# A two-layer graph network on one core: first loads issued within the preceding stage, last node tiles finished on VectorE, padding tile left out, loops written out

## What is computed

```
# layer 0: graph convolution with self loops
deg  = segment_sum(w, dst) + 1 ;  dis = rsqrt(deg)
agg  = segment_sum(x[src] * dis[src] * w, dst)      # sum0, one row per node
out0 = relu(dis * ((agg + dis * x) @ W0) + b0)
x1   = layernorm(x + out0)
# layer 1: continuous-filter convolution on edges (i = src, j = dst)
filt = (softplus(f_ij @ Wf1 + bf1) - log 2) @ Wf2 + bf2
m    = products of (x1[j] @ Win), direction Y and filt, times edge weight
agg1 = segment_sum(m @ W1, i)                       # sum1
S, V = (softplus(agg1_scalar) - log 2) @ W2_s , agg1_vector
out  = layernorm(x1 + [S, V])
```

## Time and profile before

| | us |
|---|---|
| median of three runs | 1147.39 |
| the profiled execution | 1145.88 |
| its span in the trace | 1144.1 |

### The profile page before, as it was taken

One profiled execution on the slowest core, in us unless ns is written; L12 is line 12 of the kernel. 1 busy time (PEld: TensorE's weight loads), 2 busy tenths in 40 slices (PEclk: granted clock), 3 DMA queues, 4 the chain that ended last, 5 costly groups with the idle time before them and its releaser, 6 DMA issues.

```text
span 1144.1 us, 20007 instructions
## 1 busy us (share of the span) xinstructions
PE 963.5 (84%) x4768; PEld 744.5 (65%) x4768; DVE 812.6 (71%) x2537; ACT 651.0 (57%) x1472; POOL 602.4 (53%) x692
## 2 busy tenths in 40 slices
PE   7789989999838999999994599999999999544443
PEld 7667767767627888777773477777777777333332
DVE  8888868768607787878784366666666666268887
ACT  1268867877723555555555244444445444168887
POOL 3337788888743666666665455665665664300000
PEclk9989989889978999999997699999999999855555
DMA  9989999999977999999995789999999997599994
GB/s 353 419 270 247 246 238 248 232 230 235 236 161 222 315 310 310 309 308 314 310 311 210 225 173 205 196 198 205 195 200 205 195 202 156 70 359 362 362 359 167
DMA packets 153397, 287.95 MB, mean 252 GB/s; under 512 B 17850, under 2 KB 54366, under 8 KB 153342
## 3 DMA queue, kind: packets, MB, share of 16 engines
q1 hardware_dynamic: 104254, 192.95, 49.0%
q0 software_dynamic: 35840, 83.91, 38.7%
q10 hardware_dynamic: 13248, 10.49, 2.8%
HBM read 138.88 MB, written 148.41 MB: 251 GB/s over the span
## 4 chain that ended last, share of the span: by engine, by line
PE 37%; ACT 10%; issue 9%; DVE 7%; DMA 3%; ACTq 2%; POOL 1%; DVEq 1%; SPq 1%; POOLq 0%
PE bank L1133 6%; PE bank L1144 5%; PE bank L1102 4%; DVE node_mem L880 3%; PE bank L1142 3%; PE bank L1154 3%; PE bank L1156 3%; PE bank L1157 3%; PE bank L1126 2%; ACT G_hi L618 2%; PE bank L1106 2%; ACTq L619 2%; ACT node_mem L632 2%; PE bank L1134 2%; PE bank L1140 2%
## 5 line engine op out<-in xcount | busy, mean ns | idle before, releaser
L517 POOL DMA_INDIRECT sum<-R_mem,l_sidx x80 | 127.5, 1594 | 127.1 <-ACT R_mem L646 75.0
L462 POOL DMA_INDIRECT sum<-R_mem,sidx_all x80 | 130.9, 1636 | 71.4 <-DMA sum<-zeros 34.9
L493 POOL TENSOR_TENSOR node_mem<-node_mem,G_mem 128x512 f32<-128x512 f32 x80 | 103.2, 1290 | 91.7 <-ACT node_mem L626 91.7
L1102 PE MATMUL bank<-W0h,G_hi 128*128 128x512 f32 x320 | 134.2, 419 | 0.9 <-ACT G_hi L618 0.7
L1102 PE MATMUL bank<-W0l,G_hi 128*128 128x512 f32 x320 | 126.0, 394 | 0.0
L626 ACT ACTIVATE node_mem<-node_mem 128x512 f32<-128x512 f32 x80 | 50.7, 633 | 118.1 <-DVE node_mem L880 118.1
L925 DVE SCALAR_TENSOR_TENSOR edge_mem<-edge_mem,Y,bank 128x128 f32<-128x128 f32 x240 | 72.5, 388 | 57.3 <-ACT edge_mem L660 57.3
L660 ACT COPY edge_mem<-bank 128x256 f32<-128x256 f32 x80 | 29.8, 372 | 134.3 <-PE bank L1144 134.3
L1027 PE MATMUL bank<-G_hi,M_mem 128*128 128x512 f32 x200 | 89.0, 445 | 17.4 <-ACT R_mem L561 15.9
L509 POOL DMA_INDIRECT G_mem<-x_d,dst_i x80 | 79.4, 992 | 36.8 <-issue 23.2
L1170 PE MATMUL bank<-ident,node_mem 128*128 128x128 f32 x80 | 27.5, 447 | 82.9 <-DVE node_mem L953 82.9
(11 more groups left out here) (177 smaller groups left out, 2765.6 us busy)
## 6 DMA issues: line engine op xcount, KB each, us to landing
filt_d<-node_mem SPq DMA_DIRECT2D x40, 512.0 KB, 5.0
node_mem<-sum SPq DMA_DIRECT2D x80, 256.0 KB, 3.6
G_mem<-x SPq DMA_DIRECT2D x80, 256.0 KB, 3.6
x_d<-node_mem SPq DMA_DIRECT2D x80, 256.0 KB, 2.5
node_mem<-filt_d SPq DMA_DIRECT2D x80, 256.0 KB, 4.5
sum<-zeros SPq DMA_DIRECT2D x34, 512.0 KB
sum<-node_mem SPq DMA_DIRECT2D x80, 192.0 KB, 2.8
edge_mem<-sum SPq DMA_DIRECT2D x15, 512.0 KB, 5.6
```

The lines of the kernel that those rows point to most:

```text
L462: pool.indirect_dma_start(sum0, bass.IndirectOffsetOnAxis(ap=sidx[:, t:t + 1], axis=0), R[t % 8][:, :], None, compute_op=ALU.add).then_inc ...
L493: pool.tensor_tensor(res[a], res[a], xl[a], ALU.add).then_inc(n_sum, 1)
L517: pool.indirect_dma_start(sum1, bass.IndirectOffsetOnAxis(ap=l1_sidx[:, t:t + 1], axis=0), R3[t % 8][:, :], None, compute_op=ALU.add).then ...
L1102: pe.matmul(bank[4 + a][:, :], zT_hi[a][:, c * P:(c + 1) * P], w[:, c, :], start=(c == 0 and w is W0h), stop=False)
```

## The change

- `TR` = 79 tiles are gathered, scattered and run through `nodes0` and `edges1`. The first edge stage keeps its 20 groups: TensorE, ScalarE and VectorE still work on tile 79, GpSimd neither gathers nor scatters it. `sum0`, `sum1` and `x1_d` are 128 rows shorter, and the last of the 42 zero stores has half its size.
- The first eight loads of `x` for the node stage are issued by SyncE before it waits for the filter stores and the scatters; they wait for the last low part (`e_lo`), when the `G0` buffers are free.
- The first four `trow3` and `filt` loads of the second edge stage are issued within SyncE's node stage, at step TR + 4 = 83, ahead of the store of tile 71.
- The first eight `xs` loads of the last stage are issued when the last product of the second edge stage is made, before the wait for its scatters.
- Tiles 75 to 78 of the node stage: after L880 VectorE itself applies ReLU and adds `x` in one instruction; ScalarE's ReLU and GpSimd's add are left out for them, and their statistics are taken one step earlier.
- The four DMAs of L637 are issued at steps 7, 15, 23 and 31 of ScalarE's node stage.
- `nodes0` and `edges1` are straight-line code in all steps on all engines. `held` increments nothing where its value is a number, which it now always is.
- In `edges1` tile 78 has no partner: TensorE sums it alone and ScalarE copies it one step earlier.

```diff
+TR = (N + P - 1) // P
+TAIL = TR - 4
+NR = TR * P
...
-def live(s, lag, steps=T):
+def live(s, lag, steps=TR):
...
         def held(eng, s, value):
-            if not isinstance(value, int) or value > 0:
+            if isinstance(value, int):
+                wait(eng, s, value)
+            else:
...
-            for j in range(NZ, 42):
+            for j in range(NZ, 41):
                 sp_.dma_start(zero_rows(j), zeros[:, :]).then_inc(s_zero0, 16)
+            sp_.dma_start(sum0[41 * 256:, :], zeros[:, 0:D]).then_inc(s_zero0, 16)
...
-            sp_.wait_ge(e_scat, 16 * T)
+            sp_.wait_ge(e_lo, T)
+            for t in range(8):
+                sp_.dma_start(xl[t], rows(x, t)).then_inc(n_xl[t], 16)
             for k in range(4):
                 sp_.wait_ge(w_st[k], 16 * (T // 8))
+            sp_.wait_ge(e_scat, 16 * TR)
...
                     sp_.dma_start(sl[a], rows(sum0, s)).then_inc(n_sl[a], 16)
-                    held(sp_, n_sum, s - 7)
-                    sp_.dma_start(xl[u], rows(x, s)).then_inc(n_xl[u], 16)
+                    if s >= 8:
+                        sp_.wait_ge(n_sum, s - 7)
+                        sp_.dma_start(xl[u], rows(x, s)).then_inc(n_xl[u], 16)
+                if s == TR + 4:
+                    for g in range(4):
+                        trow_in(g)
+                    sp_.wait_ge(n_tr, TR)
+                    for t in range(4):
+                        filt_in(t)
...
-            skewed(sp_, nodes0, 12, 16, unroll=8)
...
+            for s in range(TR + 12):
+                nodes0(s, s % 8)
...
-            sp_.wait_ge(f_scat, 16 * T)
+            sp_.wait_ge(f_m, K_PROD * TR)
+            for s in range(8):
+                sp_.dma_start(xs[s], node_pair(x1_d, s, 0, C)).then_inc(g_xs[s], 16)
+            sp_.wait_ge(f_scat, 16 * TR)
...
                 for n, j in enumerate((3, 2, 1, 0)):
                     t = 4 * g + j
+                    if t >= TR:
+                        continue
...
-                if live(s, 4):
+                if live(s, 4, TAIL):
                     t, a = s - 4, (u - 4) % 8
                     pool.wait_ge(n_rel, t + 1)
                     pool.tensor_tensor(res[a], res[a], xl[a], ALU.add).then_inc(n_sum, 1)
...
                     act.dma_start(sum1[bass.ds(t2 * P, P), 0:C], zeros[:, 0:C]).then_inc(s_zero1, 16)
+                    if s % 8 == 7 and s < 32:
+                        r = NR + s // 8 * P
+                        act.dma_start(sum1[r:r + P, :], zeros[:, 0:D]).then_inc(s_zero1, 16)
...
-            for q in range(4):
-                act.dma_start(sum1[NP + q * P:NP + (q + 1) * P, :], zeros[:, 0:D]).then_inc(s_zero1, 16)
...
+                stats = [t for t in (s - 6, s - 5) if live(t, 0) and (t >= TAIL) == (t == s - 5)]
+                for t in stats:
+                    if t < TAIL:
+                        dve.wait_ge(n_sum, t + 1)
+                    else:
+                        dve.wait_ge(n_add, t - TAIL + 1)
+                    dve.bn_stats(stat[t % 4][:, :], res[t % 8]).then_inc(n_bn, 1)
...
+                    if t >= TAIL:
+                        dve.wait_ge(n_pre, t + 1)
+                        dve.scalar_tensor_tensor(res[a], res[a], 0.0, xl[a], ALU.max, ALU.add).then_inc(n_add, 1)
...
+                    if t == TR - 1:
+                        pe.matmul(bank[4][:, :], M3[a][:, 0:P], msg[a][:, P:640], start=True, stop=True).then_inc(f_mm, 1)
+                    elif a % 2 == 0:
```

More of the change, by code:

```diff
@@ L465, in _ @@
                     pool.wait_ge(e_lo, 4 * (g + 1))
-                    for j in range(4):
-                        gather0(4 * g + NG + j)
+                    for t in range(4 * g + NG, min(4 * g + NG + 4, TR)):
+                        gather0(t)
             def nodes0(s, u):
-                if live(s, 7) and u % 2 == 0:
+                if live(s, 8) and u % 2 == 0:
                     t, a = s - 8, u // 2
@@ L504, in _ @@
                 if g < T2:
-                    for t in (2 * g, 2 * g + 1):
+                    for t in range(2 * g, min(2 * g + 2, TR)):
                         if t >= 8:
@@ L514, in _ @@
                         pool.wait_ge(f_scat, 32 * r)
-                    for t in (2 * r, 2 * r + 1):
+                    for t in range(2 * r, min(2 * r + 2, TR)):
                         pool.wait_ge(f_ev, t + 1)
@@ L607, in nodes0 @@
             def nodes0(s, u):
-                tail = live(s, 7) and u % 2 == 0
+                tail = live(s, 8) and u % 2 == 0
                 if tail:
@@ L633, in nodes0 @@
                        .then_inc(n_x1, 1)
[L635 to L637 removed]
+            for s in range(TR + 9):
+                nodes0(s, s % 8)
             def edges1(s, u):
@@ L668, in edges1 @@
                                    scale=Y[:, bass.ds(t, 1), 0]).then_inc(f_proj0, 1)
-            skewed(act, edges1, 8, 16, unroll=8)
+            for s in range(TR + 8):
+                edges1(s, s % 8)
             def nodes1(s):
@@ L926, in edges1 @@
                                                          bank[6][:, i * P:(i + 1) * P], ALU.mult, ALU.add))
-            skewed(dve, edges1, 6, 16, unroll=8)
+            for s in range(TR + 6):
+                edges1(s, s % 8)
             def nodes1(s):
@@ L1108, in nodes0 @@
                     ins.then_inc(n_mm, 1)
-            skewed(pe, nodes0, 3, 8)
-            pe.wait_ge(n_lo, T)
-            pe.wait_ge(n_pre, T)
+            for s in range(TR + 3):
+                nodes0(s, s % 8)
+            pe.wait_ge(n_lo, TR)
+            pe.wait_ge(n_pre, TR)
             pe.wait_ge(s_wTc, 3)
@@ L1157, in edges1 @@
                         pe.matmul(bank[7][:, :], M3[a][:, P:2 * P], msg[a][:, P:640], start=True, stop=True).then_inc(f_mm, 1)
-            skewed(pe, edges1, 7, 16, unroll=8)
-            pe.wait_ge(f_ev, T)
+            for s in range(TR + 7):
+                edges1(s, s % 8)
+            pe.wait_ge(f_ev, TR)
             def nodes1(s, u):
```

78 lines of the change are left out of this document (40 added, 38 removed).

## The result

| | before | after |
|---|---|---|
| median of four runs | 1147.12 | 1128.82 |
| ratio to before, 95% interval | | 0.9843 [0.9822, 0.9864] |
| the profiled execution | 1145.88 | 1128.47 |
| its span | 1144.1 | 1126.6 |

The change saves 18.3 us. The four runs of after lie between 1128.08 and 1131.37. In five runs on another chip the ratio was 0.9834 [0.981, 0.9858]. Two of the 17 runs of the kernel before in the first batch of experiments took 1312.76 and 1676.30 at a granted clock of 0.725 and 0.565, and no ratio counts them; without them that batch's median of 1143.94 is 1143.34.

A forecast was written before the change was run, and what follows sets the result against it. GpSimd paces the first edge stage, ScalarE/VectorE rings the node and last stages, TensorE the second edge stage, whose end waits for scatters. 4.8 + 3.4 + 5.5 + 1.2 + 1.35 + 1.9 = 18.2, so 1147.39 becomes 1129.2; range 1121.5 to 1135.

The forecast's parts named there:

- the unchanged turns: Node stage: two turns of the ScalarE and VectorE ring stay at 6.76 us, 3.38 a tile, with loops written out.
- parts 1 and 2: End of the first edge stage (-2.3 us) and first loads of the node stage (-2.5): together -4.8.
- rival (d): Both written-out stages: straight-line code feeds queues late, 0.30 us a step, costing 47, so 1176; chance 0.04.
- part 4: Tail of the node stage: gather 5.5 us earlier without the tile's 3.4 (ends 3.5 and 7); first gather's landing -1.2.
- the stores behind them have caught up by 614: Node stage's tail: stores behind the eight early loads (3.7 us at about 607) catch up six microseconds before the last.
- the increments: Ten waits before the second edge stage's first gather lose one increment each; last store to gather taken 3.9 us, before 5.43.
- The cover that the text named: Node stage's tail: stores catch up after the second edge stage's eight early loads; without that cover these cost 3.7 us.
- Part 1: End of the first edge stage: tile's scatter -1.86, gather -1.4, zero stores -0.3, load burst +1.3; sum -2.3 us, ends -4.4 and 0.
- a last scatter that lands over 7.5: Stated sign that the forecast is wrong: a last scatter landing over 7.5 us after its issue.
- Rival (a): Joints after both edge stages: early loads slow the scatters by what they save; 13.9 us saved, 1133.5; chance 0.11.
- Rival (b): Stage joints: loads are hidden anyway, data rate or the compute behind decides; 14.1 us saved, 1133.3; chance 0.08.
- Part 5: End of the second edge stage: tile's scatter issue -1.86, early x1_d loads +0.5; sum -1.35 us.

## Why the prediction was right, point by point

"First profile" is the difference of the two profiled executions shown above; "over the runs" takes means over all kernels that share the step, except the first row, which is the one kernel with the tile put back and for which other pairs give 0.2 to 3.8.

| step of the prediction | forecast | first profile | over the runs |
|---|---|---|---|
| last scatter of edge stage 1 issued | -3.55 | -2.99 | -3.1 |
| its landing beside the loads of x | +1.3 | +2.64 | +1.3 |
| first load to first matmul | -3.0 | -2.75 | -2.6 |
| slow clock in the first tiles | +0.5 | -0.36 | -0.2 |
| node stage, one tile less, to the last aggregate | -3.4 | -4.67 with the next | -3.2 |
| finish, to the last aggregate | -0.75 | | -1.2 |
| last aggregate to last store | -3.2 | -2.75 | -2.6 |
| last store to gather | -1.5 | +0.33 | +0.2 |
| landing of the first gather | -1.2 | -2.86 | -2.8 |
| edge stage 2 to first load of the last | -1.35 | -1.46 | -2.1 |
| last stage | -1.9 | -2.63 | -2.0 |
| sum | -18.05 | -17.50 | -18.3 |

That the sum came out within 0.1 of the measured 18.3 is luck: in the first profile single parts missed by up to 1.8 one way and 1.7 the other, and cancelled. In the same way the last column adds up to 18.3 from means that are each uncertain by some tenths, the first by more than 1, so its agreement proves nothing.

**Right, with its mechanism.** The tile, the unchanged turns, the written-out loops at nothing, the finish on VectorE (617.1 was forecast for the aggregates of tile 78; shifted by the 4.8 of parts 1 and 2 that is 612.3, it was 613.1; from VectorE's low part of tile 77 it is 11.5 forecast and 11.2 measured), the first matmul 6.9 behind the first load (6.60), and the last stage's 8.8 (8.48). The fetching of straight-line code, for which rival (d) stood, costs nothing that can be measured over the 128 steps that were a loop before: 0.9997, where 0.12 a step would have given 1.013. The Trainium skill ("Runtime: NRT & Kernel Launch", Instruction fetch mechanics) says sequential code is fetched ahead, mostly hidden; this run agrees, and the taken branches of the loop, which by that section can stall, cost nothing that this run can tell either.

**Failed in part 4: "the stores behind them have caught up by 614".** The issues had: SyncE's queue is in step again before the last stores (616.50 and 617.14). The data had not. The prediction looked at the queue's issues, 0.46 apart, and not at the bytes: 1.5 MB is 3.75 us of engines that were to be nearly full with stores and loads anyway, and they were busy over nine tenths until 3.3 us after the last issue. So the step from last store to gather gained nothing, where 1.5 was forecast, and of the two causes that should have shortened it one (the zero stores moved away, some 2.2 by the kernels above) was used up by the early loads, and the other (the increments) was worth nothing. The cover that the text named, and priced at 3.7 if gone, was gone for 2.4 of it.

**Too small in the same part: the landing of the first gather.** 4.9 was taken between 3.55 and 6.1; with the early loads out of its way it is 3.25 to 3.52 in every kernel. The row nearest in kind was the one with nothing beside it, and the text left it for a middle value. These two misses have opposite signs and the same cause: the 1.5 MB, 3.75 us of transfer at 400 GB/s, cost 2.4 where they run into the last stores (5.7 for 3.3) and 3.2 where they run into the first gather (6.6 for 3.4).

**Part 1** ended outside its condition in the first profile ("a last scatter that lands over 7.5"), at 8.29, so that only 0.35 of 2.3 was left there. It was the size of one term in one execution, in which the burst ended only 2.0 ahead of the last scatter: the mean over eight profiles is 7.11 and the term 1.3, as forecast, but two of the eight lie over 7.5 (8.29 and 8.06). The forecast took one number for what depends on how the filter stores and the scatters fall together. The rule in the Trainium skill that queue rows take turns ("DMA: Bandwidth & Descriptors", Queues, rings and completion order), by which the burst would cost nearer 3, has the direction right; its size is nearly met by two profiles of eight (2.5 and 2.2). Four loads cost nothing, which neither the rule nor the term had. Rival (a), the loads cost what they save, was half true at this joint (1.3 of 2.6) and nearly true at the third (1.2 of 1.5); at the second, 2.4 and a last store issued 0.4 later stand against 3.2. The three together are still worth 2 to 4 us. Rival (b), loads hidden anyway, fails at all three joints: with the loads early, what stands behind them came 2.6, 3.2 and 1.5 sooner than with them late.

**Part 5** took 0.5 for the loads of `x1_d` beside the scatter; they cost 1.2. It took 1.86 for the tile; it is worth about 3.1. Part of the rest is that the stage now ends with the landing of a scatter alone, 4.6 to 4.9 behind its issue, where the second of a pair took 5.0 to 5.3; some 0.8 stays unexplained. The two errors cancel in the first profile (-1.5 for -1.35), so that row alone would have passed for a confirmation.

(The forecast was given as 18.2; its parts were rounded one by one.)

## What to carry to other kernels

Before a first load is moved ahead of the preceding stage's last stores or scatters, count its bytes against what the DMA engines have left there: the queue's issues can be back in step while the data are microseconds behind. Take the transfers that the next step needs and no more, spread the small ones over the steady steps, and take bulk that belongs nowhere in particular, such as zeroing, away from the joint: the moved zero stores, as far as the traces tell, were worth about as much here as all the early loads together. And when a joint comes out as forecast, look at its parts, since a burst moved across a landing shortens one and lengthens the other by like amounts.

## What the runs showed of the hardware that was not expected

- Eight plain loads (2 MB on one queue) issued around the first of three accumulating scatters made the last one land 1.3 later in the mean and 0.3 to 2.5 in single executions, the more the later the burst ended (7.4 to 8.3 where it ended 1.7 to 2.0 ahead of that scatter, 6.1 where 4.6); four of them, 1 MB, cost nothing (5.83 and 5.85 beside 5.84 with none).
- Stores and loads between HBM and the core's memory ran at 373 to 421 GB/s for 8 us on end in the kernel after.
- With these engines full, over 612 to 626 in the kernel after, stores of 256 and 192 KB took 4.8 and 5.1 from issue to landing (medians), and most of SyncE's issues 0.56 to 0.71 each; with gaps between transfers, in the kernel with the loads put back, 2.1 and 2.3, and 0.32 to 0.46.
- TensorE stood at full clock over 348 to 352, from 1.9 behind its first matmul (0.56 in the same window before, whose first matmul was at 349.16): transposes had begun at 343.17 already, and the earlier start cost no clock: from the first matmul to the fourth high part it took 5.4 in the mean of the eight kernels with eight early loads of `x`, 5.6 in the four with none.
